# A two-layer transformer on one core: idle TensorE products at the stage seams, and the first score maxima taken as a + relu(b - a)

## What is computed

```python
h = _modulate(_layernorm(x), shift_msa, scale_msa)
qkv = (h @ W_qkv + b_qkv).reshape(b, l, 3, H, D)
scores = jnp.einsum('blhd,bmhd->bhlm', q * scale, k)
attn = jax.nn.softmax(scores, axis=-1)
o = jnp.einsum('bhlm,bmhd->blhd', attn, v).reshape(b, l, c)
x = x + gate_msa * (o @ W_proj + b_proj)
h = _modulate(_layernorm(x), shift_mlp, scale_mlp)
mlp = jax.nn.gelu(h @ W_fc1 + b_fc1, approximate=True) @ W_fc2 + b_fc2   # layer 0
moe = jnp.einsum('te,etc->tc', cw, eo)                                    # layer 1
```

## Time and profile before

| | |
|---|---|
| median of 3 runs | 1550.79 us (1545.91 to 1553.46) |
| the profiled execution: time, span | 1542.11 us, 1540.4 us |
| PE, DVE, ACT, POOL busy | 90%, 72%, 53%, 41% of the span |
| mean granted TensorE clock | 0.929 |

### The profile page before, as it was taken

How to read it: one execution, slowest core, us unless ns; L and a number is a source line. 1 busy time by engine, 2 the same in 40 slices (tenths; PEclk the granted TensorE clock), 3 DMA queues, 4 the chain that set the end, 5 groups by cost and what they waited for, 6 DMA issues and landing times. The chain is left out here.

```text
span 1540.4 us, 27402 instructions
## 1 busy us (share of the span) xinstructions
PE 1392.7 (90%) x9863; PEld 852.2 (55%) x9863; DVE 1114.8 (72%) x1807; ACT 811.8 (53%) x1533; POOL 631.9 (41%) x870
## 2 busy tenths in 40 slices
PE   5989999999997889989799999999986499999995
PEld 3753333333333678967433333333345499999994
DVE  3557899999991646766589999999839365666653
ACT  3623778877885431245157877877851133333331
POOL 2145433553000435534479877988005212121121
PEclk7975999999998989989679999999998699999998
DMA  7576434544001178427743211330039577676773
GB/s 188 164 188 111 116 85 110 137 108 72 3 3 33 51 229 281 162 57 241 172 60 50 48 32 23 48 49 3 4 131 341 186 231 206 206 233 183 240 197 77
DMA packets 93836, 194.63 MB, mean 126 GB/s; under 512 B 35734, under 2 KB 63448, under 8 KB 90716
## 3 DMA queue, kind: packets, MB, share of 16 engines
q1 hardware_dynamic: 61802, 117.93, 24.2%
q0 software_dynamic: 31600, 73.00, 21.5%
q10 hardware_dynamic: 306, 2.00, 0.6%
HBM read 127.27 MB, written 66.68 MB: 126 GB/s over the span
## 5 line engine op out<-in xcount | busy, mean ns | idle before, releaser
L1099 DVE TENSOR_REDUCE att_neg_max<-att_for_max 128x1 f32<-128x1024 f32 x512 | 617.1, 1222 | 52.6 <-PE att_for_max L1177 47.1
L1084 ACT ACTIVATE att_probs<-att_scores 128x512 f32<-128x512 f32 x1002 | 541.8, 604 | 173.5 <-PE att_scores L1216 166.0
L1228 PE MATMUL att_out<-att_probs,V 128*32 128x256 f32 (+1 forms) x3232 | 310.5, 456 | 2.9 <-ACT att_OZ L1070 1.9
L1177 PE MATMUL att_for_max<-att_KS,att_QS 54*128 54x512 f32 x640 | 243.3, 455 | 6.8 <-DVE att_neg_max L1099 6.8
L1216 PE MATMUL att_scores<-att_QS,att_KS 56*128 56x512 f32 x618 | 225.4, 450 | 0.9 <-DMA att_QS<-att_neg_max_rows 0.9
L2093 ACT ACTIVATE experts_gelu<-experts_proj,experts_b 128x256 f32<-128x256 f32 x171 | 81.1, 474 | 207.9 <-PE experts_proj L2162 186.1
L1177 PE MATMUL att_for_max<-KS,QS 54*128 54x512 f32 x384 | 165.5, 530 | 13.2 <-DVE att_neg_max L1099 10.1
L2162 PE MATMUL experts_proj<-experts_x_parts,w_parts 128*128 128x256 f32 (+1 forms) x1197 | 173.6, 285 | 1.4 <-DVE experts_x_parts L1902 1.4
L2051 POOL DMA_INDIRECT sums_of_experts<-experts_y,experts_rows x38 | 61.2, 1610 | 259.4 <-DVE experts_y L1938 253.6
L1216 PEld LDWEIGHTS att_scores<-att_QS,att_KS 56*128 56x128 f32 x618 | 94.3, 184 | 131.4 <-ACT att_probs L1084 115.2
L2162 PEld LDWEIGHTS experts_proj<-experts_x_parts,w_parts 128*128 128x128 f32 (+1 forms) x1197 | 157.4, 190 | 5.4 <-issue 5.4
(11 more groups left out here) (267 smaller groups left out, 1980.5 us busy)
## 6 DMA issues: line engine op xcount, KB each, us to landing
w_parts<-w_parts SPq DMA_DIRECT2D x19, 2304.0 KB
qk_halves<-qkv_qk_parts SPq DMA_DIRECT2D x40, 288.0 KB
w_parts<-w_parts SPq DMA_DIRECT2D x4, 2592.0 KB, 26.1
slot_rows<-mlp_blank_rows SPq DMA_DIRECT2D x2, 5145.0 KB
att_QS<-qk_halves POOLq DMA_DIRECT2D x120, 72.0 KB, 4.6
att_KS<-qk_halves POOLq DMA_DIRECT2D x60, 144.0 KB, 5.2
w_parts<-w_parts SPq DMA_DIRECT2D x19, 432.0 KB
experts_rows<-slot_rows SPq DMA_DIRECT2D x19, 294.0 KB, 10.3
```

Of the source, the lines that this page charges most:

```text
L1084: nc.scalar.activation(PR[st % 2][:, j, :], score_bank(st, n), ACT.Exp, scale=SCALE).then_inc(exp_done, 1)
L1099: nc.vector.tensor_reduce(negm[half][:, c:c + 1], psM[ring % 2][:].rearrange("p a n -> p (a n)"), AX_X, ALU.max, negate=True).then_inc(rin ...
L1177: last = nc.tensor.matmul(psM[ring % 2][:, keys, :], QS[s][rows, half, p, t * P:(t + 1) * P], KS[s][rows, p, keys * BLK:(keys + 1) * BLK], ...
L1228: last = nc.tensor.matmul(psO[32 * j:32 * j + 32, n0:n1], T.V[:, g, k, 32 * j:32 * j + 32], PR[st % 2][:, j, n0:n1], start=(k == 0 and n0 ...
```

## The change

Two parts. First, `keep_busy` issues products whose result nobody reads, 512 columns each (the matrix `sel_parts` against itself, repeated four times), into an unused bank: 4 ahead of and 3 behind the first transposes of each qkv stage, 12 at the end of each attention stage, 24 ahead of the last block's transposes and 6 at the end of the projection stage, 10 at the end of the MLP stage, and 16 in the experts stage, once the scatter of the last tile but one has been issued, ahead of the first `turn_rows`.

Second, the 20 units of a head from the third on are computed another way. With a the scores of the first 512 keys and b those of the last 512, max(a, b) = a + relu(b - a). TensorE makes b - a in one bank (a product with the second keys and one with the negated first keys, `minus`), and a in another; ScalarE takes relu of the difference into SBUF (`gains`, two buffers); VectorE does one `tensor_tensor_reduce` over 512 columns: add, negate by the scale, and reduce by min. The ring of the head has three entries (the third in `psS[2]` and `psO`). The step part keeps the two-entry ring and the plain reduction. PE and ACT wait for all 23 ring entries of the head before the first score and the first exp. In layer 0 the four copies of ScalarE move behind the relu of unit 5.

```diff
@@ -35,6 +35,7 @@
 NBLK = TOKENS // BLK
 HALVES = SEQ // BLK
 EPS = 1e-6
+LARGEST = 3.0e38
 SCALE = float(D) ** -0.5
 HG = 4
 GPB = H // HG
@@ -123,6 +124,13 @@
         return sems[-1]

     return sb, banks, sem
+
+
+def keep_busy(nc, T, bank, n):
+
+    many = T.sel_parts[:].rearrange("p (o n) -> p o n", o=1).broadcast_to([P, 4, P])
+    for _ in range(n):
+        nc.tensor.matmul(bank.rearrange("p (o n) -> p o n", o=4), T.sel_parts[:], many, start=True, stop=True)


 CK = C // 3
@@ -741,7 +749,9 @@
         def _(pe):
             pe.sem_inc(N.xt_ready, KC)
             pe.sem_inc(N.xn_ready, 1)
+            keep_busy(nc, T, psV[0][:], 4)
             norm_transposes(nc, pe, N, T, psT, 0, T.xn0[l])
+            keep_busy(nc, T, psV[0][:], 3)
             pe.wait_ge(w_ready, KC)


@@ -856,7 +866,7 @@
         full = sb("inverse", [P, HG * BLK // P], F32)
         inv = [sb(f"inverse_parts{s}", [P, 2, HG * BLK // P], F32R) for s in range(HALVES)]
         RR = [sb(f"inverse_rows{s}", [P, BLK], F32R) for s in range(HALVES)]
-        last = sb("last_inverse", [P, BLK], F32)
+        last = PR[0][:, 0, :]
         if pieces:
             S = Splitter(nc, T, pieces, sb("w_f32", [P, FF], F32), [sb(f"w_parts{n}", [P, 2, FF], F32R) for n in range(2)],
                          sem)
@@ -896,6 +906,23 @@
         wide_in = sem("wide_in")
         plus_added = sem("plus_added")

+        diff_ready = sem("diff_ready")
+        gain_ready = sem("gain_ready")
+        minus_ready = sem("minus_ready")
+        minus = sb("minus_keys", [P, PAIRS, BLK], F32R)
+        gains = [PR[1][:, n, :] for n in range(2)]
+        PLAIN, HEAD_SLOTS = 2, 3
+        HEAD_ITEMS = UNITS + AHEAD + 1
+
+        def head_item(q):
+            return q + (q > UNITS + 1)
+
+        def head_banks(n):
+
+            if n % HEAD_SLOTS < 2:
+                return psM[n % HEAD_SLOTS][:, 0, :], psM[n % HEAD_SLOTS][:, 1, :]
+            return psS[2][:], psO[:]
+
         arow = PR[0][0:B].rearrange("p j n -> p (j n)")
         psA, psC = psS[0], psS[1]
         spread_rows = [(T.gate[1][:, 0], 2), (T.gate[1][:, 1], 5), (T.mrow[:, 0], 3), (T.mrow[:, 1], 4)]
@@ -1069,11 +1096,20 @@
                     act.wait_ge(ring_read, divided[span - HALVES])
                 nc.scalar.activation(OZ[span % HALVES][:], psO[:], ACT.Copy).then_inc(oz_ready, 1)

+            nc.scalar.activation(minus[:], T.KS0[:, :, 0:BLK].bitcast(F32), ACT.Copy, scale=-1.0).then_inc(minus_ready, 1)
+            for q in range(PLAIN, UNITS + AHEAD):
+                n = head_item(q)
+                act.wait_ge(diff_ready, q - PLAIN + 1)
+                if q >= PLAIN + 2:
+                    act.wait_ge(ring_read, head_item(q - 2) + 1)
+                nc.scalar.activation(gains[q % 2], head_banks(n)[1], ACT.Relu).then_inc(gain_ready, 1)
+                if early and q == ROWS_AT[-1]:
+                    act.wait_ge(rows_ready, 1)
+                    for a in range(NA):
+                        nc.scalar.activation(arow[:, a * AW:(a + 1) * AW], psA[32 * a:32 * a + B, 0:AW], ACT.Copy
+                                             ).then_inc(rows_out, 1)
+            act.wait_ge(ring_read, HEAD_ITEMS)
             if early:
-                act.wait_ge(rows_ready, 1)
-                for n in range(NA):
-                    nc.scalar.activation(arow[:, n * AW:(n + 1) * AW], psA[32 * n:32 * n + B, 0:AW], ACT.Copy
-                                         ).then_inc(rows_out, 1)
                 act.wait_ge(row_stored, 16)
                 act.wait_ge(cols_ready, 1)
             for st in range(STEPS):
@@ -1102,7 +1138,7 @@

             def max_rows(span):
                 nonlocal ring
-                turn = psM[ring % 2][0:UNITS, 0, 0:P]
+                turn = (psM[ring % 2][:, 0, :] if span else head_banks(ring)[0])[0:UNITS, 0:P]
                 dve.wait_ge(ring_ready, ring + 1)
                 if span:
                     dve.wait_ge(m_loaded[(span - 1) % HALVES], 64 * ((span - 1) // HALVES + 1))
@@ -1138,8 +1174,23 @@
                 nc.vector.tensor_tensor(T.O[:, g, half * BLK:(half + 1) * BLK], OZ[half][:], last[:], ALU.mult
                                         ).then_inc(ring_read, 1)

+            def head_max(q):
+                nonlocal ring
+                g, half, i, p, t = unit_at(q)
+                c = i * UNITS // 2 + p * TPB + t
+                here = head_banks(ring)[0]
+                dve.wait_ge(ring_ready, ring + 1)
+                dve.wait_ge(gain_ready, q - PLAIN + 1)
+                nc.vector.tensor_tensor_reduce(out=here, in0=here, in1=gains[q % 2], scale=-1.0, scalar=LARGEST,
+                                               op0=ALU.add, op1=ALU.min, accum_out=negm[half][:, c:c + 1]
+                                               ).then_inc(ring_read, 1)
+                ring += 1
+
             for q in range(UNITS + AHEAD):
-                reduce(q)
+                if q < PLAIN:
+                    reduce(q)
+                else:
+                    head_max(q)
                 if q == UNITS + 1:
                     max_rows(0)
                 if early and q == MOD_AT:
@@ -1182,9 +1233,13 @@

             def turn(span):
                 nonlocal ring
-                ring_free()
+                if span:
+                    ring_free()
+                else:
+                    head_free()
                 pe.wait_ge(ring_read, maxima[span])
-                nc.tensor.transpose(psM[ring % 2][0:UNITS, 0, 0:P], negm[span % HALVES][:], T.ident[:]
+                at = (psM[ring % 2][:, 0, :] if span else head_banks(ring)[0])[0:UNITS, 0:P]
+                nc.tensor.transpose(at, negm[span % HALVES][:], T.ident[:]
                                     ).then_inc(ring_ready, 1)
                 ring += 1

@@ -1231,9 +1286,28 @@
                 if n1 == BLK:
                     last.then_inc(pv_done, 1)

-            def unit(q):
-                max_half(q, 0)
-                max_half(q, 1)
+            def head_free():
+
+                if ring >= HEAD_SLOTS:
+                    pe.wait_ge(ring_read, ring - HEAD_SLOTS + 1)
+
+            def head_unit(q):
+                nonlocal ring
+                g, half, i, p, t = unit_at(q)
+                rows = slice(i * LANES, i * LANES + ROWS)
+                queries = T.QS0[rows, half, p, t * P:(t + 1) * P]
+                first, second = (T.KS0[rows, p, keys * BLK:(keys + 1) * BLK] for keys in range(2))
+                head_free()
+                if q == PLAIN:
+                    pe.wait_ge(minus_ready, 1)
+                here, other = head_banks(ring)
+                if q >= PLAIN:
+                    nc.tensor.matmul(other, queries, second, start=True, stop=False)
+                    nc.tensor.matmul(other, queries, minus[rows, p, :], start=False, stop=True).then_inc(diff_ready, 1)
+                else:
+                    nc.tensor.matmul(other, queries, second, start=True, stop=True)
+                nc.tensor.matmul(here, queries, first, start=True, stop=True).then_inc(ring_ready, 1)
+                ring += 1

             def ada(q):

@@ -1252,13 +1326,14 @@
                         last.then_inc(cols_ready, 1)

             for q in range(UNITS + AHEAD):
-                unit(q)
+                head_unit(q)
                 if early:
                     ada(q)
                 if q == UNITS + 1:
                     turn(0)
             if early:
                 pe.wait_ge(cols_out, 1)
+            pe.wait_ge(ring_read, HEAD_ITEMS)
             for st in range(STEPS):
                 units = list(units_of(st))
                 plain = span_turned(st) is None and span_behind(st, SPREAD_LAG) is None
@@ -1288,6 +1363,7 @@
             ring_free()
             nc.tensor.matmul(psM[ring % 2][:, 0, :], T.sel[:], OZ[HALVES - 1][:], start=True, stop=True
                              ).then_inc(ring_ready, 1)
+            keep_busy(nc, T, psO[:], 12)


 def project_stage(nc, T, l, W):
@@ -1299,6 +1375,7 @@
         N = Norm(sb, sem)
         psT = banks("xT", KC)
         psP = banks("proj", TPB)
+        psF = banks("idle", 1)[0]

         proj_ready = sem("proj_ready")
         added = sem("added")
@@ -1417,7 +1494,10 @@
             for i in range(NBLK):
                 if i + 1 < NBLK:
                     project(i + 1)
+                else:
+                    keep_busy(nc, T, psF[:], 24)
                 norm_transposes(nc, pe, N, T, psT, i)
+            keep_busy(nc, T, psF[:], 6)


 def mlp_stage(nc, T, l, W, pieces, following):
@@ -1584,6 +1664,7 @@
                     down(k - LAG)
             for k in range(NBLK * NF - LAG, NBLK * NF):
                 down(k)
+            keep_busy(nc, T, psH[0][:], 10)


 ROUTED = [(0, 3), (3, 5), (8, 5), (13, 3)]
@@ -1699,6 +1780,7 @@
         route_steps = sem("route_steps")
         filled = sem("rows_filled")
         row_out = sem("row_out")
+        nearly_out = sem("nearly_out")
         w2_in = sem("w2_in")
```

(8 more changed lines are left out.)

## The result

The changed kernel takes 1536.07 us, the kernel before 1550.04 us, medians of four runs each: ratio 0.9912, 95% interval 0.9885 to 0.9938. Two later comparisons on other chips gave 0.9949 (0.9918 to 0.9981) and 0.9929 (0.9905 to 0.9953).

What follows compares the result with a forecast made beforehand. VectorE's maxima were taken to bound steady attention and the heads, half clock the steps behind layer 1's head. Heads -12.0 and idle products -5.4 took 1542.1 to 1524.7 us profiled, 1533 as median; range 1525 to 1551.

Steps and rivals of the forecast that it cites:

- The new VectorE instruction, 0.75 us: Heads: each new VectorE reduction over 512 columns takes 0.75 us, between 0.69 from below and 1.22 from above.
- The rivals of 1.22 us and of a slow reduction: Heads' new reduction takes 1.22 us or a little more: 1542 us, chance 0.14; or 1.9 us: 1569 us, chance 0.10.
- the second rival: Heads: new reduction costs 1.22 us or a little more, gain only 1.6 to 2 us a layer: 1542 us, chance 0.14.
- A unit turn of 0.90 us at half clock: Heads: 2.7 us per ring entry over three entries; fifteen layer 1 units at 0.90 instead of 1.27 save 5.5 us.
- I expect full clock after a few units: 7.0 us: Layer 1's head: denser products raise the clock, saving 7.0 us, between 5.5 at 0.90 and 8.0 at 0.74 a unit.
- the rival on this point: Clock stays at half in the heads: -5.4 us in layer 1, -1.5 in layer 0; 1539 us, chance 0.17.
- From the split of the maxima to their landing it takes 4.2 us: End of layer 1's head: this time, read from the old trace, stays 4.2 us, so earlier maxima bring an earlier first score.
- The last four units need 3.0 to 3.6 us, so the new wait for all 23 entries is hidden in it: End of the head: the wait for all ring entries ends within the 4.2 us landing and costs nothing.
- Layer 0, -5.0, bounds -5.2 and -1.5: Layer 0's head: maxima come 5.2 us earlier at full clock, 1.5 at half; -5.0 taken.
- End of attention and end of projection: -4.8: 12 idle products give -2.4 us at three chances in four; 24 give -1.1, and -1.3 in the MLP at even chance.
- Start of qkv: 0: The 4 and 3 idle products at the start of qkv gain nothing; bounds -1.5 and +1.2 us a layer.
- Products in the way: Rival: clock falls before the idle products, which then overrun at the seams and gain nothing: 1546 us, chance 0.09.

Runs made afterwards that it cites:

- two slots: Changed kernel with the head's ring at two entries instead of three: 1547.81 us, one run.
- a hold: Changed kernel, group 1's loads waiting for the first maxima: all held 1547.40 us; second half, with late broadcasts and pairs, 1531.65; that plus idle products before heads, 1529.05.

## Why the prediction was right, and where it was not

The direction and the time were right: faster, 1536 against 1533 us. The sum behind it was not. From the profiles, the heads brought 3.6 us and not 12; the idle products brought 5.9 and not 5.4: together 9.5 us, not 17.4. The forecast took 17.4 from the median of before; the first comparison showed 14.0 there, more than the profiles account for and more than the two later ones (7.3 and 10.7), and this is why the forecast fell close. That is luck: the forecast is a ratio of 0.989, inside the first interval and below the whole of the two later ones. The steps that failed are all in the heads.

- *The new VectorE instruction, 0.75 us.* Mis-sized by little and harmless: 0.70 and 0.14 us, but back to back a new one starts every 0.66 us, and VectorE does not bind. The rivals of 1.22 us and of a slow reduction are out, and so is what I made of the accumulator: 0.84 us for both rows is far from the second rival. The Trainium skill, "VectorE: DVE Perf Modes", on two Vector instructions with no wait between them, counts an op that writes its accumulator as two instructions; the trace agrees, the second is the 0.14 us row.
- *A unit turn of 0.90 us at half clock.* Right in layer 1: 0.94 (2.81 us for three), and two slots gave 1.41, by the same chain 2.7 / 2 = 1.35. The split moved by 5.65 us, where the half-clock branch said 5.5.
- *"I expect full clock after a few units: 7.0 us".* Failed. All of layer 1's head ran at half clock in every run with three slots, but for its first 1 to 3 us in some; the rival on this point was right. A term of 1.5 us.
- *"From the split of the maxima to their landing it takes 4.2 us."* This is the step that failed most. It held in layer 1 only because the loads of group 1 had landed when the slow head had finished (22.8 us after the first product, the split at 24.4). POOL begins to issue them some 6 to 8 us after the stage's first product, 753 to 763 us in layer 1, whatever the head does, and earlier maxima land behind them: 6.1 to 7.2 us. In the three heads of layer 1 with a hold it is 4.7 to 4.9. Of the 5.65 us, 1.9 to 2.9 are given back. The Trainium skill, "DMA: Bandwidth & Descriptors", on queues, rings and completion order, says that each DMA engine takes its queues in turn, a whole packet at a time. The traces agree so far as four transfers of 4 KB land 2 to 4 us later beside POOL's loads; whether the turns are the reason, no run here shows.
- *"The last four units need 3.0 to 3.6 us, so the new wait for all 23 entries is hidden in it."* Failed, at a small price. At half clock the last entry is read 4.24 us after the split in layer 0 and 4.5 in layer 1, not before the landing of 4.2. In eight of the ten heads of layer 0 with three slots the profile puts the last wait before the first score down to it, my own sign of being wrong. It cost 0.1 us there (4.34 against 4.24), since the landing was hardly shorter.
- *Layer 0, -5.0, bounds -5.2 and -1.5.* Measured -0.3, outside my bounds. At half clock the split moved by 0.2 to 0.7 us only, since TensorE has the modulation's products between the units as well and is busy for 26.2 of 26.7 us. Of that, the transposes that split the pairs of units cost 1.5 us, by the run that keeps them. When the clock was full for the first 10 us, it moved by 3.6 and the landing took 8.0.
- *The first plain reduction 0.4 earlier, exp's table late in layer 1.* Both seen: 1.26 instead of 1.64 us, and the load at 771.57. The fourth exp comes 3.6 us after the score instead of 2.6; by the 16th nothing is left of it.
- *End of attention and end of projection: -4.8.* Measured -4.4. In the first profile the projection's first products ran at full clock. They do not always: over the eleven profiles with these 12 products the clock fell to half at the start of the projection in 10 of 22 cases. In layer 1 the projection takes 33.5 us where it held (six profiles, all three of the kernel after among them) and 35.2 us, as before, where it did not. My chance of three in four was too high, and part of the -1.5 us is luck. The gap of 7.39 us was covered, and the stretch ended on the same ScalarE row.
- *Start of qkv: 0.* Together -1.2, within the bounds: +1.1 in layer 0 and -2.3 in layer 1 with the 10 products at the MLP's end. Which of the two sets brings the 2.3 us was not separated.
- *Products in the way.* Not seen at the ends of attention, projection and MLP, where they ran at full clock (mean 0.39 to 0.43 us each). At the experts they ran partly at half (0.50 us), with 5.38 us of waiting left behind them. At the start of qkv in layer 0 the +1.1 us may be theirs; there the clock was at half.

The rows of the two seams behind the kernel after's 24 and 16 products, with what TensorE waited for next:

```profile
532.18 5.76 PE L133 MATMUL proj_idle<-sel_parts 128*128 128x512 f32 x24
539.48 1.09 PE L445 MATMUL proj_xT<-ident,proj_x_normed 128*128 128x128 f32 x8 [1.54 <-ACT proj_x_normed L432]
...
1196.18 5.26 PE L133 MATMUL experts_proj<-sel_parts 128*128 128x512 f32 x16 [7.13 <-DVE experts_gone L1954]
1206.82 1.11 PE L2228 MATMUL experts_turned<-ident,experts_rows 128*128 128x128 f32 x4 [5.38 <-DMA experts_rows<-slot_rows]
```

What stays open: how much of the first comparison's 14 us is chance; what ends the clock at the start of one projection and not of another; and why holding half of group 1 back costs layer 1 4 us in one run and 7 to 11 in the other, of which one wait of 2.5 to 2.9 us was found. A fix that orders POOL's weight loads behind the second span's maxima was not tried.

## What to carry to other kernels

A latency that is read in the old trace holds for the old timing. Before work is moved forward in time, look at what the shared DMA engines do at its new time, not at its old one. When the bound engine gets a cheaper instruction, count the load of the next one with everything that is interleaved there: in layer 0 the modulation's products fill TensorE, and the new head gave next to nothing. Idle products that are to fill a wait must be counted at half clock, or they become the wait. And where run-to-run spread is as large as the parts, compare stages in several profiles before medians of parts.

## What the runs showed of the hardware

The granted clock stayed at half through 18.7 us in which TensorE was busy for 18.55, all products with 54 rows. Entering the head at full clock, it fell 1.2 to 3.2 us into it in layer 1 (six heads) and 0.5 to 10.2 us into it in layer 0. With seven products of 128 rows in the landing it was back at the first score (from 764.0 to 767.4 it fell once more) in layer 1 and 1.8 us behind it in layer 0, against 9 us behind the score of layer 1 without them. The runs do not tell whether the rows are the cause or something else that differs between these products.

A wait of 4.8 us for four transfers of 4 KB was seen where they were issued 0.05 us beside a 576 KB load, and none where they were issued 5.2 us ahead of it. Layer 0's steps took 321 to 327 us in the five profiles without such a wait and 327 to 336 us in the nine with one. Four of those five also have the idle products ahead of the heads, so the two are not taken apart. The wait could be much of the spread from run to run; it was seen only in profiled executions, one for each run.
